# A macaron block on one NeuronCore: the second attention's output projection in two-part float16, and one of seven running sums moved from GpSimd to VectorE

## What is computed

```
x = x + 0.5 * int8_ffn(layernorm(x))            # step 0
x = x + attention_0(layernorm(x))               # step 1: 16 heads of 8, causal, rotary
x = x + 0.5 * int8_ffn(layernorm(x))            # step 2
x = x + 0.5 * gated_ffn(layernorm(x))           # step 3
x = x + attention_1(layernorm(x))               # step 4: 16 heads of 64, causal
x = x + 0.5 * gated_ffn(layernorm(x))           # step 5

def attention_1(x):                             # w_q, w_k, w_v: 16 x 64 x 128; w_o: 1024 x 128
    q, k, v = x @ w_q.T, x @ w_k.T, x @ w_v.T   # per head
    a = softmax(causal(q @ k.T / 8))
    return concat(a @ v) @ w_o
```

## Time and profile before

| | us |
|---|---|
| median of 3 runs | 767.06 (766.93 to 768.41) |
| the profiled execution's own time | 767.2 |
| its span, first to last instruction | 765.1 |

### The profile page before, as it was taken

How to read it: one execution, slowest core, us unless ns; L and a number is a source line. 1 busy time by engine, 2 the same in 40 slices (tenths; PEclk the granted TensorE clock), 3 DMA queues, 4 the chain that set the end, 5 groups by cost and what they waited for, 6 DMA issues and landing times.

```text
span 765.1 us, 21672 instructions
## 1 busy us (share of the span) xinstructions
PE 702.7 (92%) x9399; PEld 423.5 (55%) x9399; DVE 539.6 (71%) x773; ACT 434.0 (57%) x542; POOL 484.1 (63%) x385
## 2 busy tenths in 40 slices
PE   2768988898888899999999999999999999999997
PEld 1523535445444463666655575655777655666674
DVE  7598897989988985786777566757345776552286
ACT  2325576988777769545555654564725456646311
POOL 6824455405854400389999899957758796989910
PEclk9855799999999999999999999999999999999999
DMA  8000000000000000001011101100010101111000
GB/s 282 2 1 2 3 2 3 2 4 3 3 2 3 2 3 2 2 3 30 3 29 30 30 3 30 31 20 13 30 30 2 31 3 30 30 30 30 2 29 27
DMA packets 13013, 15.66 MB, mean 20 GB/s; under 512 B 3000, under 2 KB 10488, under 8 KB 12920
## 3 DMA queue, kind: packets, MB, share of 16 engines
q1 hardware_dynamic: 12344, 13.96, 6.3%
q10 hardware_dynamic: 576, 0.33, 0.1%
HBM read 12.74 MB, written 1.16 MB: 18 GB/s over the span
## 4 chain that ended last, share of the span: by engine, by line
PE 60%; DVE 14%; POOL 13%; ACT 7%; issue 5%; DMA 0%; POOLq 0%; ACTq 0%; DVEq 0%
PE ps L1330 15%; PE ps L1279 12%; DVE big L1130 8%; ACT Pr L740 6%; POOL V0s L723 6%; PE ps L1249 5%; PE ps L1496 5%; PE ps L1309 5%; POOL acts L723 4%; PE ps L1535 3%; PE ps L1503 3%; PE ps L1445 2%; PE ps L1340 1%; PE ps L1453 1%; PE ps L1465 1%
## 5 line engine op out<-in xcount | busy, mean ns | idle before, releaser
L740 ACT ACTIVATE Pr<-ps 128x1024 f32<-128x1024 f32 (+1 forms) x249 | 225.4, 955 | 102.9 <-PE ps L1330 43.0
L1161 DVE TENSOR_REDUCE mxb<-ps 128x8 f32<-128x1024 f32 x145 | 172.4, 1212 | 78.4 <-PE ps L1330 47.1
L1130 DVE TENSOR_REDUCE big<-ps 128x8 f32<-128x1024 f32 (+1 forms) x163 | 170.6, 1093 | 22.0 <-PE ps L1309 14.9
L723 POOL TENSOR_TENSOR V0s<-V0s,Pr 128x1024 f32<-128x1024 f32 x58 | 136.7, 2356 | 76.5 <-ACT Pr L740 48.7
L1330 PE MATMUL ps<-big 64*128 64x128 f16 (+2 forms) x2560 | 168.0, 259 | 0.4 <-ACT Pr L740 0.2
L1309 PE MATMUL ps<-big 32*128 32x128 f16 (+2 forms) x1280 | 102.5, 279 | 29.8 <-DVE big L1130 15.7
L1330 PEld LDWEIGHTS ps<-big 64*128 64x128 f16 x2560 | 93.0, 94 | 61.0 <-issue 20.3
L1309 PEld LDWEIGHTS ps<-big 32*128 32x128 f16 x1280 | 43.3, 96 | 103.0 <-ACT Pr L740 39.8
L1279 PE MATMUL ps<-Pr,V1s 128*64 128x128 f32 (+2 forms) x732 | 81.7, 365 | 0.0
L1249 PE MATMUL ps<-Pr,V0s 128*18 128x128 f32 (+2 forms) x1280 | 80.5, 376 | 0.7 <-ACT Pr L747 0.7
L723 POOL TENSOR_TENSOR acts<-acts,Pr 128x1024 f32<-128x1024 f32 x26 | 61.3, 2358 | 9.3 <-PE ps L1279 5.9
(11 more groups left out here) (252 smaller groups left out, 1029.0 us busy)
## 6 DMA issues: line engine op xcount, KB each, us to landing
rec_b<-scratch_dram SPq DMA_DIRECT2D x28, 256.0 KB, 3.9
X<-in_x_dram SPq DMA_DIRECT2D x2, 256.0 KB, 3.5
big<-in_pick_rows_dram SPq DMA_DIRECT2D x2, 256.0 KB, 3.2
X<-in_x_dram SPq DMA_DIRECT2D x1, 512.0 KB, 5.2
rec_b<-in_w_q_dram SPq DMA_DIRECT2D x1, 512.0 KB, 5.7
XT<-in_w_k_dram SPq DMA_DIRECT2D x1, 512.0 KB, 6.5
XT<-in_w_v_dram SPq DMA_DIRECT2D x1, 512.0 KB, 7.3
wo_s<-in_w_o_dram SPq DMA_DIRECT2D x1, 512.0 KB, 8.1
```

Source lines behind the costliest of these rows:

```text
L723: g.tensor_tensor(dst, dst, src, ALU.add).then_inc(summed, 1)
L740: ins = a.activation(dst[:, part], src, func, scale=scale)
L1130: ins = v.tensor_reduce(maxima_of(mall[:, r, 2 * u:2 * u + 2][:, part], i), block_view(src, i), AX.X, ALU.max, negate=True)
L1161: ins = v.tensor_reduce(maxima_of(mxb[:, r][:, part], arg), block_view(src, arg), AX.X, ALU.max, negate=True)
```

## The change

1. **Projection in two-part float16.** `wo` makes three float16 matmuls (`PARTS`) where it made one float32 matmul. Its operands are made new: `wo1_16` from w_o (a fourth `Square`, a fourth `wsplit` step with one ScalarE and two GpSimd instructions, and a scale by a power of two as q, k and v have), and `Y16` from `y`: GpSimd normalises `y_raw` in place, ScalarE copies it to float16 (the high part) after exp place 5 of the second pair after it, and VectorE subtracts (the low part) at place 7; for the last pair these are places 3 and 4. `save_y` and `wo` wait for the low part instead of for `normed`. The projection is scaled back in VectorE's addition (L1182), and v no longer is in its copy.
2. **First of seven sums by VectorE.** GpSimd adds six chunks a pair, VectorE adds the first, at the place of weigh step 2. GpSimd's additions wait for it (`first_added`).
3. **The ring has 7 buffers** instead of 8 (six in `Pr` and `more_buf`).
4. **A new string.** Its second half differs most around `wo` and at the end. At its beginning, `ln` step 0 of the second sequence (VectorE's `bn_stats` L1072) stands ahead of the first `gkq`, where it stood behind 22 `gmax` steps. In the second half, `ln` step 1 of norm (3, 1), GpSimd's part, stands behind 24 exponential steps where it stood behind 28 (those are pair 3's first), and some turns and sums trade places.

```diff
+POOL_ADDS = ADDS - 1
+ADD_AT = 2
-CHUNK_BUFS = 8
+CHUNK_BUFS = 7
+Y_HIGH_AT, Y_LOW_AT = (5, 3), (7, 4)
+SCALED = 2, 4
...
-              + [("wsplit", n, None, "") for n in range(3)] + middle_steps(0) + ...
+              + [("wsplit", n, None, "") for n in range(4)] + middle_steps(0) + ...
...
 ORDER = (
-    "ammmmmmmmmammmmmmmmmmmtammheehemehwemmhweemememwewemewmemwmmwememhemehmemwthehawm..."
+    "hammmmmmmmmmmmmhmammmmmmtmmmeehmememeeemwmheweemwmmeemamewmemwemewehemmhtmmwhemwe..."
...
# GpSimd
-                if p == 0:
-                    pool.wait_ge(slot_filled, filled("gkq", G - 1, None))
-                if p >= NP:
-                    pool.wait_ge(slot_filled, filled("wo", 0, (0, NP, WO_PARTS - 1)))
-                g.tensor_tensor(YT[:, p % NP], y_raw[p % 2], rec_b[:], ALU.mult).then_inc(normed, 1)
+                g.tensor_tensor(y_raw[p % 2], y_raw[p % 2], rec_b[:], ALU.mult).then_inc(normed, 1)
...
-                    if arg < BASE or (key, arg) == (LAST, CH - 1):
+                    if place_of(key, arg) <= BASE or (key, arg) == (LAST, CH - 1):
                         continue
...
-                    pool.wait_ge(pv1, CH * p + BASE)
+                    pool.wait_ge(first_added, p + 1)
...
# ScalarE
-                    act.wait_ge(normed, p - 1)
+                    act.wait_ge(y_low, p - 1)
                 a.activation(y_raw[p % 2], banks(6, 2), ACT.Copy).then_inc(acc1_saved, 1)
...
+                    if place_of(key, arg) == Y_HIGH_AT[key == LAST] and key >= 2:
+                        done = key - 2
+                        act.wait_ge(normed, done + 1)
...
+                        a.activation(Y16[:, 0, done % NP], y_raw[done % 2], ACT.Copy).then_inc(y_high, 1)
...
# VectorE
+                if kind == "exp" and place_of(key, arg) == Y_LOW_AT[key == LAST] and key >= 2:
+                    done = key - 2
+                    dve.wait_ge(y_high, done + 1)
+                    v.tensor_tensor(Y16[:, 1, done % NP], y_raw[done % 2], Y16[:, 0, done % NP], ALU.subtract).then_inc(y_low, 1)
+                if kind == "weigh" and place_of(key, arg) == ADD_AT:
+                    c = chunks_of(key)[BASE]
+                    dve.wait_ge(slot_act, read("A", "exp", key, c))
+                    dve.wait_ge(pv1, CH * key + BASE)
...
+                    v.tensor_tensor(dst, dst, src, ALU.add).then_inc(first_added, 1)
...
# TensorE, wo
-                    pe.wait_ge(normed, key * NP + last)
-                    pe.wait_ge(wo1_in, 16)
+                    pe.wait_ge(y_low, key * NP + last)
+                    pe.wait_ge(w_split, 4)
                     for m in range(first, last):
                         for t in range(2):
-                            ins = te.matmul(slot[0][:, tile(t)], YT[:, m, tile(2 * k + t)], wo1_s[:, m],
-                                            start=m == first and t == 0, stop=m == last - 1, skip_group_check=True)
+                            for part, (ww, yy) in enumerate(PARTS):
+                                ins = te.matmul(slot[0][:, tile(t)], Y16[:, yy, m, tile(2 * k + t)], wo1_16[:, ww, m],
+                                                start=(m, t, part) == (first, 0, 0), stop=(m, part) == (last - 1, 2),
+                                                skip_group_check=True)
```

More of the change, by code:

```diff
@@ L209, in streams @@
         "h": (first_steps(1) + [("scale", 1, None, "V")]
-              + [("wsplit", n, None, "") for n in range(3)] + middle_steps(0) + middle_steps(1) + gated_steps(5, 0)),
+              + [("wsplit", n, None, "") for n in range(4)] + middle_steps(0) + middle_steps(1) + gated_steps(5, 0)),
     }
 ORDER = (
-    "ammmmmmmmmammmmmmmmmmmtammheehemehwemmhweemememwemewmemwmmwememhemehmemwthehawmheewehmewmegemewmemme"
-    "wmemwmmhmemewemhmmeweehmtmwmemwmhhhhmhmememwmeemewemgemhehmhwemhwmeehwemamewememtemwemememwmemwemwem"
@@ L321, in macaron_block_kernel @@
         moments = sb("moments", [P, T, 6])
-        wmax = [sb(f"wmax_{k}", [P, 2 + k]) for k in range(2)]
-        wsum = [sb(f"wsum_{k}", [P, 2 + k]) for k in range(2)]
-        qk_scale = [sb(f"qk_scale_{k}", [P, 2 + k]) for k in range(2)]
-        v_back = sb("v_back", [P, 1])
+        wmax = [sb(f"wmax_{k}", [P, SCALED[k]]) for k in range(2)]
+        wsum = [sb(f"wsum_{k}", [P, SCALED[k]]) for k in range(2)]
+        qk_scale = [sb(f"qk_scale_{k}", [P, SCALED[k]]) for k in range(2)]
+        y_times, y_back = sb("y_times", [P, 1]), sb("y_back", [P, 1])
         exp_scale = [sb(f"exp_scale_{k}", [P, 1]) for k in range(2)]
@@ L333, in macaron_block_kernel @@
         wo1_s = sb("wo1_s", [P, NP, P])
+        wo1_16 = sb("wo1_16", [P, 2, NP, P], F16)
+        more_buf = sb("more_buf", [P, 1024])
         wg_s = sb("wg_s", [P, 2, HID], F16)
@@ L359, in macaron_block_kernel @@
         X1 = XT1[:, :, :].rearrange("p b s -> p (b s)").bitcast(F16).rearrange("p (b w s) -> p b w s", b=B, w=2)
-        w_raw = [rec_b[:], XT1[:, 0], XT1[:, 1]]
+        w_raw = [rec_b[:], XT1[:, 0], XT1[:, 1], wo1_s[:].rearrange("p n c -> p (n c)")]
+        w_parts = [[wqkv1[:, n, w] for w in range(2)] for n in range(3)] + [
+            [wo1_16[:, w].rearrange("p n c -> p (n c)") for w in range(2)]]
         cs = wkqv_s[0:2 * T, 0:2 * P].rearrange("p (r c) -> p r c", r=2)
@@ L390, in macaron_block_kernel @@
         sums_s = [big[:, 15360 + 512 * r:15360 + 512 * (r + 1)] for r in range(2)]
-        YT = big[:, 0:8192].rearrange("p (n s) -> p n s", n=NP)
-        chunk_buf = [by_head(at) for at in buf[0:6] + [late_buf[:, r] for r in range(2)]]
+        Y16 = big[:, 0:8192].bitcast(F16).rearrange("p (w n s) -> p w n s", w=2, n=NP)
+        chunk_buf = [by_head(at) for at in buf[0:6] + [more_buf[:]]]
         Psum = [by_head(V0s[:, 0:2 * S]), by_head(V0s[:, 2 * S:4 * S]),
@@ L716, in _ @@
                     pool.wait_ge(slot_act, READS["A"][n])
-                    pool.wait_ge(pv1, CH * p + BASE)
-                    if g_no:
-                        pool.wait_ge(summed, g_no)
+                    pool.wait_ge(first_added, p + 1)
+                    before = POOL_ADDS * p + place_of(p, arg) - BASE - 1
+                    if before:
+                        pool.wait_ge(summed, before)
                     dst, src = summed_columns(total, arg), chunk_buf[g_no % CHUNK_BUFS]
@@ L867, in _ @@
                         act.wait_ge(w_in, 16 * W_LOADS)
-                        for k in range(3):
-                            if k == 2:
-                                act.wait_ge(wmax_ready, 2)
+                        act.wait_ge(wo1_in, 16)
+                        for k in range(4):
+                            if k >= 2:
+                                act.wait_ge(wmax_ready, k)
                             a.activation(ffn_h[:, k % 2], w_raw[k], ACT.Square,
@@ L913, in _ @@
                     act.wait_ge(sums_in, 16 * (key - 1))
-                    copy_out(n, sums_s[key % 2][:, 256 * arg:256 * arg + 256], slot[0][:, 0:256])
+                    act.wait_ge(slot_filled, SLOT_NO[n] + 1)
+                    a.activation(sums_s[key % 2][:, 256 * arg:256 * arg + 256], slot[0][:, 0:256], ACT.Copy,
+                                 scale=y_by).then_inc(slot_act, 1)
                 if kind == "lwo" and key == LAST:
                     act.wait_ge(pv1, CH * LAST + (FIRST_HALF, CH)[arg])
-                    act.wait_ge(normed, LAST - 1)
+                    act.wait_ge(y_low, LAST - 1)
                     a.activation(y_raw[LAST % 2][:, half_of(arg)], bank(ACC1[arg]), ACT.Copy).then_inc(last_saved, 1)
@@ L1402, in _ @@
                 if kind == "scale":
-                    pe.wait_ge(wmax_ready, 4)
-                    ins = te.matmul(slot[0][:, 0:2 + key], ones_s[:], wmax[key][:], start=True, stop=True)
+                    pe.wait_ge(wmax_ready, 5)
+                    ins = te.matmul(slot[0][:, 0:SCALED[key]], ones_s[:], wmax[key][:], start=True, stop=True)
                 if kind == "xq":
```

64 lines of the change are left out of this document (39 added, 25 removed).

## The result

| kernel | median us | runs | ratio to the kernel before, 95% interval |
|---|---|---|---|
| before, beside it | 767.73 | 4 | 1 |
| changed | 781.15 | 4 | 1.0148 [1.0123, 1.0172] |

The change makes the kernel 1.5% slower, where 1% faster was forecast. The profiled execution took 779.7 us, with a span of 777.9 us.

What follows compares the result with a forecast made beforehand. TensorE was taken to bound the second attention, with GpSimd also full from 672 to 722 us. The terms -6.4 - 1.5 + 1.5 + 0.5 - 0.8 = -6.7 gave 760.4 us, range 755.5 to 769.0 (the forecast's own: 758 to 762).

Steps and rivals of the forecast that it cites:

- The projection's -6.4 us: Projection steps on TensorE: 0.92 us saved in each of four, 0.68 in each of four more; bounds -5.0 and -6.4.
- 2.0 forecast there: Tail: three of the second sequence's four projection steps are on its chain and give 2.0 us.
- the cost of VectorE's added work: Second attention: about 37 us more on VectorE, mostly covered by its 166 us of idle time from 300 to 722 us.
- 17 to 25 us, of which I take 17: VectorE's 14 low-part subtractions with two SBUF inputs: at least 1.23 us each, 17 us taken in all.
- the +1.5 us charged for it: Second attention: charge for all of VectorE's and ScalarE's added work and the ring of 7; bounds 0 and +16.3.
- 0 (where it is idle) to 1.07 us: What each of the 30 new VectorE instructions costs GpSimd in collisions, together up to 32 us.
- up to 32 had been allowed: Upper limit in us of GpSimd's loss to 30 collisions, leaving 8 to 17 of its 40 us relief.
- GpSimd's relief, -1.5 us: Sixteen additions, 40 us, leave GpSimd; worth only TensorE's waits for it, bounds 0 and -2.5, -1.5 us taken.
- the two waits by which it was priced: TensorE's waits for GpSimd's additions: 1.0 us before 420 us and 1.5 us before 721 us.
- +0.5 - 0.8 = -0.3: First stage: +0.5 us for the fourth square, copy and split; -0.8 us for the moved `bn_stats`.
- The slower one: Rival: ScalarE's high copy waits 16.3 us for GpSimd's normalisation, 7.8 us reach TensorE, 768.2 us; chance 0.14.
- the first rival: GpSimd stays as full as it was, as all 30 collisions with VectorE cost 1.07 us: 762.6 us; chance 0.20.

Runs made afterwards that it cites:

- x1: The changed kernel with the string of the kernel before, the fourth split's letter put behind the third's: 807.08 us, 1.0497 to before.
- x15: The kernel before, own string with the fourth split's letter added, with the float16 projection, all seven sums on GpSimd and a ring of 7: 799.88 us, 1.0414.
- x2: The kernel before with the new string alone, without the fourth split's letter: 790.93 us, 1.028 to before.
- x10: The kernel before, ring of 7, with 14 extra VectorE maxima of one SBUF input that nobody waits for: 769.08 us, 0.9981.
- x9: The kernel before, ring of 7, with 14 extra VectorE subtractions of two SBUF inputs that nobody waits for: 777.65 us, 1.0082.
- x3: The changed kernel with VectorE's low-part subtraction replaced by a one-input maximum; the third product reads the high part: 773.29 us, 1.005 to before.
- x8: The kernel before with the new string, the ring of 7 and the first sum on VectorE, projection in float32: 774.38 us, 1.0058.
- x13: The changed kernel with the last pair's low part moved right behind the first sum: 779.92 us, 1.0148 to before.
- x12: The kernel before, own string and float32 projection, with a ring of 7 and the first sum on VectorE: 783.13 us, 1.0147.
- x11: The changed kernel with ten pairs' low parts directly ahead of the first sum and their high copies at an earlier exponential: 792.09 us, 1.0269.
- x5: The changed kernel with its string's first 468 letters from the kernel before, plus the fourth split's: 787.57 us, 1.0228 to before.

## Why the prediction was wrong

**The projection's -6.4 us** was right as TensorE's work: the steps have the forecast lengths. As time it came only in part: the old string's tail shortens by 1.2 us (x1 and x15, of 2.0 forecast there), the new string's doesn't shorten (40.0 us; 39.7 with that string alone, x2).

**The failed step is the cost of VectorE's added work** ("17 to 25 us, of which I take 17", and the +1.5 us charged for it). The prediction saw the collisions, but priced them "0 (where it is idle) to 1.07 us" on GpSimd's side alone and let VectorE's own 1.23 us hide in its idle time. The runs show that hiding holds for one input (x10: nothing) and not for two (x9: +8.8 us; x3 against the changed kernel: 7.0 us). VectorE is held for up to 2.1 us at a time, and behind it stand the maxima that free TensorE's banks: TensorE's waits for them rise from 1.0 us in x10 to 5.3 in x9. The 14 low parts lost 14 x (1.95 - 1.22) = 10.2 us so, the 16 first sums 15.7 + 7.4 - 16 x 1.22 = 3.6. The side that was priced is the smaller one: GpSimd's 95 additions lost some 8 us in all, where up to 32 had been allowed.

**GpSimd's relief, -1.5 us**, failed as well: the two waits by which it was priced are gone, but new string and first sum together give +2.7 us of the stretch (x8). The runs can't divide these 2.7 us further. What the rows show is that GpSimd's sums now begin when VectorE has made its first one, and that in the tail, where its queue is full, GpSimd idles 3.61 us for it.

**The sum by the stretch.** New string and first sum +2.7 (forecast -1.5), projection without its collisions -1.6 (x3 against x8; forecast -6.4 + 1.5 = -4.9), its collisions +7.0 (forecast 0): +8.1 against -6.4. In the middle term the tail is 0.8 us longer where 2.0 us less were forecast, for which the chain through the high copy is the cause read in the rows; of it x13 tried one link and got 0.9 us back. The rest of the term agrees within 0.5 us.

**The first stage** was forecast at +0.5 - 0.8 = -0.3. The profiles put its end 4.7 us later, but the kernels x9, x10 and x12, which change next to nothing before it, end it 4 to 6 us later than the profile of before too. Taking each median less its kernel's stretch and the 2 us around the span, x9, x10 and x12 have 313 to 314 us, the changed kernel 317: an estimate of +4 us. With the stretch's +8.1 this makes some 12 us, beside the 11.4 us that the ratio of 1.0148 gives. The clock doesn't explain it: from 38 to 300 us the granted clock is 0.91 in the changed kernel, and 0.88 to 0.89 in x9, x10 and x12. Its likely cause, TensorE's 5 us of longer waits for the maxima, is read from two profiles and was not tried by itself.

**The rivals.** The slower one (ScalarE held by the high copy) is real but small here: 7.8 us of waits, longest 3.2, against the 16.3 us that it went through. In other orders it is larger (x1, x11, x15), and TensorE's waits for ScalarE there, 10.5 to 20.9 us, are among the longest. What made the kernel slower was the mechanism of the first rival, on the side that it left out. GpSimd's wait for the first sum and the layer norm queued behind it, which the prediction had at nothing, cost TensorE 7.0 us at one place in x12, about half of its 13.7.

**Open:** why the granted clock rises later in x5 and x15 than in x1 after the same wait of TensorE, and how the first stage's +4 us come about.

## What to carry to other kernels

Moving an elementwise operation from GpSimd to VectorE, or adding one there, is not free even on an idle VectorE as long as it has two SBUF inputs and GpSimd works beside it: price each engine's operation at its length plus the rest of the other's that it meets, and look at who stands behind it. In these runs an operation with one SBUF input hid, and so did one that ran while GpSimd waited, as far as nothing new waited for it. A hand-written order is part of each variant: an edit is to be judged in its own order and in the old one, since the same first sum was worth 15 us in one and cost 14 in the other. Before a handed-over operation is added in a full stretch, follow the chain of engines that it joins (here GpSimd, ScalarE, VectorE, GpSimd) and count the idle time at each link.

## What was not expected of the hardware

In the rows shown the two engines exclude each other completely, and both ways: with 0.19 us between the starts, VectorE's 1.22 us became 3.25, and GpSimd's next 2.36 us became 3.12. It goes with VectorE's second input from SBUF: at an offset of 0.67 us a subtraction took 2.77 us (x9) and a maximum of one input 1.21 us (x10), beside additions of 2.36 and 2.37 us, and an operation with one input from SBUF, one from PSUM and a full output to SBUF kept its 1.22 us (`L1176`).
